# Projection and routing: where the scale and shift of the second normalisation are applied

## What is computed

```python
mod = (silu(c) @ wmod).reshape(8, 6, 1, 512)         # sa, ca, ga, sb, cb, gb per sequence
h = layernorm(x) * (1 + ca) + sa
x = x + ga * attention(h)                            # 16 heads, causal, with output projection
h = layernorm(x) * (1 + cb) + sb                     # the h of this document
shared = relu2(h @ shared_up.T) @ shared_down.T      # 512 -> 1024 -> 512
scores = sigmoid(h @ gate_w.T)                       # 32 experts, 4 chosen per token
routed = sum over the 4 chosen experts of weight * relu2(h @ up[e].T) @ down[e].T
x = x + gb * (routed + shared)
```

## Time and profile before

| | |
|---|---|
| median of 3 runs | 3025.01 us (3016.74 to 3033.07) |
| span of the profiled execution, first to last instruction | 3027.5 us |
| PE busy | 2895.4 us, 96% |
| PEld busy | 2168.3 us, 72% |
| DVE busy | 2179.3 us, 72% |
| POOL busy | 1833.5 us, 61% |
| ACT busy | 1341.6 us, 44% |

### The profile page before, as it was taken

How to read it: one execution, slowest core, us unless ns; L and a number is a source line. 1 busy time by engine, 2 the same in 40 slices (tenths; PEclk the granted TensorE clock), 3 DMA queues, 4 the chain that set the end, 5 groups by cost and what they waited for, 6 DMA issues and landing times.

```text
span 3027.5 us, 49806 instructions
## 1 busy us (share of the span) xinstructions
PE 2895.4 (96%) x16480; PEld 2168.3 (72%) x16480; DVE 2179.3 (72%) x5344; ACT 1341.6 (44%) x2436; POOL 1833.5 (61%) x1077
## 2 busy tenths in 40 slices
PE   8999999999999999999999989999999999989997
PEld 5788888766666666666666677777777787767775
DVE  6555555678787878787877687777777787756664
ACT  2222222156666666666666522233222333226664
POOL 1233222278888888888886256766565666655664
PEclk9999999999999999999999999999999999999998
DMA  7655555756655665566555333332322322238996
GB/s 240 211 187 201 187 180 180 233 114 136 137 124 115 138 138 121 115 139 140 119 117 160 107 97 93 94 112 74 103 79 93 102 85 81 73 107 222 239 245 118
DMA packets 281948, 420.53 MB, mean 139 GB/s; under 512 B 48463, under 2 KB 132687, under 8 KB 281742
## 3 DMA queue, kind: packets, MB, share of 16 engines
q1 hardware_dynamic: 259214, 384.22, 44.9%
q0 software_dynamic: 22528, 33.72, 5.8%
HBM read 263.38 MB, written 153.01 MB: 138 GB/s over the span
## 4 chain that ended last, share of the span: by engine, by line
PE 53%; DVE 14%; POOL 14%; issue 8%; ACT 4%; DMA 4%; another core or an unknown queue 2%; DVEq 1%; POOLq 0%; SPq 0%; ACTq 0%
PE qkv_ps_m L840 12%; PE ffn_ps_m L2191 11%; POOL att_gathered L1105 6%; PE qkv_ps_m L844 6%; POOL att_pt L1098 5%; PE att_ps_o L1330 5%; PE att_ps_p L1386 4%; PE att_ps_s L1304 4%; DMA out<-exp_y,exp_tok_add 2%; PE exp_ps_u L1607 2%; PE exp_ps_y L1623 1%; PE att_ps_s L1361 1%; DVE ffn_att L147 1%; DVE ffn_x L149 1%
## 5 line engine op out<-in xcount | busy, mean ns | idle before, releaser
L247 DVE CUSTOM_DVE_ANT_0 att_ps_s<-att_ps_s,att_causal 128x512 f32<-128x512 f32 (+1 forms) x992 | 469.3, 502 | 175.5 <-PE att_ps_s L1304 171.3
L1166 ACT ACTIVATE att_pt<-att_ps_p 128x512 f32<-128x512 f32 (+1 forms) x1024 | 524.5, 589 | 143.6 <-PE att_ps_p L1389 110.2
L1304 PE MATMUL att_ps_s<-att_ks,att_qs 96*128 96x512 f32 x1488 | 513.4, 373 | 2.2 <-DVE att_lower L253 0.6
L1386 PE MATMUL att_ps_p<-att_qs,att_ks 98*128 98x512 f32 (+3 forms) x1536 | 498.5, 364 | 9.3 <-ACT att_pt L1166 8.0
L1098 POOL TENSOR_TENSOR att_pt<-att_pt 128x1024 f32<-128x1024 f32 (+2 forms) x153 | 331.1, 2164 | 166.6 <-PE att_ps_o L1330 144.8
L1105 POOL TENSOR_TENSOR att_gathered<-att_gathered,att_pt 128x2048 f32<-128x2048 f32 (+1 forms) x92 | 388.1, 4218 | 7.2
L1912 POOL DMA_INDIRECT slot_info<-ffn_info,ffn_slot x256 | 275.9, 1078 | 119.3 <-issue 76.5
L253 DVE TENSOR_REDUCE att_lower<-att_ps_s 128x1 f32<-128x512 f32 x496 | 339.2, 684 | 7.4 <-PE att_ps_s L1304 7.4
L1386 PEld LDWEIGHTS att_ps_p<-att_qs,att_ks 98*128 98x128 f32 x1536 | 272.6, 191 | 82.1 <-issue 34.7
L1304 PEld LDWEIGHTS att_ps_s<-att_ks,att_qs 96*128 96x128 f32 x1488 | 275.7, 191 | 73.3 <-DVE att_rowmax L247 27.7
L577 POOL TENSOR_TENSOR qkv_x<-qkv_x,qkv_mod 128x512 f32<-128x512 f32 x60 | 83.4, 1391 | 371.5 <-DVE qkv_x L671 371.5
(11 more groups left out here) (311 smaller groups left out, 6718.8 us busy)
## 6 DMA issues: line engine op xcount, KB each, us to landing
att_qs<-qk_parts SPq DMA_DIRECT2D x96, 512.0 KB, 6.8
att_ks<-qk_parts SPq DMA_DIRECT2D x96, 512.0 KB, 12.7
qk_parts<-qkv_out_hi SPq DMA_DIRECT2D x128, 256.0 KB, 2.2
qk_parts<-qkv_out_lo SPq DMA_DIRECT2D x128, 256.0 KB, 2.4
qkv_x<-x SPq DMA_DIRECT2D x16, 1024.0 KB, 5.6
v_rows<-qkv_out_v SPq DMA_DIRECT2D x64, 256.0 KB, 2.3
att_vs<-v_rows SPq DMA_DIRECT2D x32, 512.0 KB, 16.1
o_parts<-att_o SPq DMA_DIRECT2D x64, 256.0 KB, 7.9
```

The lines of the kernel that those rows point to most:

```text
L247: dve.tensor_tensor_reduce(part, part, self.causal[:, UNIT - (c1 - c0):UNIT], scale=1.0, scalar=MASKED, op0=ALU.add, op1=ALU.max, accum_ou ...
L1166: act.activation(tile(c)[:, h, col:UNIT], ps_p[(NPROB * prev.g + n) % NP][:, col:UNIT], ACT.Exp, scale=float(HD) ** -0.5).then_inc(exp_don ...
L1304: pe.matmul(bank("s", cur.g, i)[:, 0:c1 - c0], qs[cur.slot][0:STACK, h, t * P:(t + 1) * P], ks[cur.slot][0:STACK, h, c0:c1], start=True, s ...
L1386: last = pe.matmul(part[:, i * (UNIT - col):(i + 1) * (UNIT - col)], ks[prev.slot][:, h + i, kt * P:(kt + 1) * P], qs[prev.slot][:, h + i, ...
```

## The change

TensorE turns rows that are only normalised. ScalarE then scales and shifts the turned tile in its PSUM bank, where a feature is a partition, so `1 + cb` and `sb` are one column each per block of 128 features (four activations a tile, `modulated`), and copies it to `hT_hi` as before. GpSimd multiplies and shifts all four tiles of `h2` behind their turns, for the store to DRAM alone. VectorE's part of that for the last tile goes, and in `norm_first` for all four.

With this the order is changed: GpSimd does `normalise(u + 2)` ahead of `modulate`, and `scatter` in one piece; SyncE stores `h2` of unit u at the start of the body of u, ahead of the wait for the projection and of loading the attention output; the columns `mod_cols` are loaded element by element for every sequence; tiles 0 and 1 are turned behind the second down tile, tile 2 behind the third, and the last one at pair 2 of the last down tile.

```diff
-LINKS = 2 * UT + 1 + STAT_LINKS + ROOT_LINKS + 2
+LINKS = 2 * UT + 1 + STAT_LINKS + ROOT_LINKS
+MOD_FIRST, MOD_EACH = 48, 80
...
             def load_rows():
 
-                for m, j in enumerate((M_GA, M_CB, M_SB)):
-                    sp.dma_start(bridge.mod[:, m, :], mod_dram[0:1, j, :].broadcast_to([P, D])).then_inc(late.mod_in, 16)
+                sp.dma_start(bridge.mod[:, 0, :], mod_dram[0:1, M_GA, :].broadcast_to([P, D])).then_inc(late.mod_in, 16)
+                for m, j in enumerate((M_CB, M_SB)):
+                    sp.dma_start(bridge.mod_cols[:, m, :], mod_dram[0:1, j, :].rearrange("o (k p) -> p (o k)", p=P),
+                                 allow_slow_non_contiguous=True).then_inc(late.mod_in, 16)
...
             def norm_first():
 
                 late.deviation(dve, 0, 0, bridge.mv, bridge.std, bridge.rstd, bridge.tmp)
                 for t in range(UT):
-                    last = dve.tensor_scalar(late.h2[:, t, :], late.x0[:, t, :], bridge.mv[:, t, 0:1], bridge.rstd[:, t:t + 1],
-                                             ALU.subtract, ALU.mult)
...
+                    dve.tensor_scalar(late.h2[:, t, :], late.x0[:, t, :], bridge.mv[:, t, 0:1], bridge.rstd[:, t:t + 1],
+                                      ALU.subtract, ALU.mult).then_inc(late.norm_done, 1)
...
-        TURNS = ((), (0,), (1, 2), ())
-        SCATTERED_AHEAD = TOPK
+        TURNS = ((), (0, 1), (2,), ())
+        LAST_TURN = 2
...
             def store_h2(b, half):
                 u = b * HALVES + half
-                sp.wait_ge(h_done, CREDIT + PT * (u + 1))
-                sp.wait_ge(norm_done, CREDIT + UT * (u + 1))
+                sp.wait_ge(h_done, CREDIT + UT * (u + 1))
...
                 if more:
-                    nb, nhalf = (b, 1) if half == 0 else (b + 1, 0)
...
-                        sp.wait_ge(proj_done, CREDIT + UT * (u + 2))
-                        load_o(b + 1, half)
-                    store_h2(nb, nhalf)
-                    if half == 0 and has_next2:
-                        load_mod(b + 1)
+                    store_h2(b, half)
+                if more and half == 1:
+                    sp.wait_ge(hi_done, CREDIT + UT * (u + 1))
+                    load_mod(b + 1)
+                if b < LAST:
+                    sp.wait_ge(proj_done, CREDIT + UT * (u + 2))
+                    load_o(b + 1, half)
...
             def modulate(b, half):
                 u = b * HALVES + half
-                for t in range(PT):
-                    pool.wait_ge(norm_done, CREDIT + UT * u + t + 1)
+                pool.wait_ge(mod_in, CREDIT + MOD_FIRST + MOD_EACH * (b + 1))
+                pool.sem_inc(mark, 1)
+                for t in range(UT):
+                    pool.wait_ge(tr_done, CREDIT + UT * u + t + 1)
...
             def body(b, half, more):
                 u = b * HALVES + half
-                if u == UNITS - 2:
-                    scatter(u, half, 0, SCATTERED_AHEAD)
+                if b < LAST:
+                    normalise(u + 2)
+                if u >= UNITS - 2:
+                    scatter(u, half)
                 if more:
                     modulate(*((b, 1) if half == 0 else (b + 1, 0)))
-                if half == 0 and not (isinstance(b, int) and b == LAST) or half == 1 and more:
-                    normalise(u + 2)
-                scatter(u, half, SCATTERED_AHEAD if u == UNITS - 2 else 0, UT * TOPK)
+                if u < UNITS - 2:
+                    scatter(u, half)
...
-            def turn(u):
-
+            def turn(u, cols):
+
+                act.wait_ge(mod_in, CREDIT + MOD_FIRST + MOD_EACH * (u // HALVES + 1 if u else 0))
                 for t in range(UT):
                     act.wait_ge(tr_done, CREDIT + UT * u + t + 1)
+                    for k in range(DK):
+                        part = ps_t[t % 2][:, k * P:(k + 1) * P]
+                        last = act.activation(part, part, ACT.Identity, bias=cols[:, 1, k:k + 1], scale=cols[:, 0, k:k + 1])
+                    last.then_inc(modulated, 1)
+                    act.wait_ge(modulated, CREDIT + UT * u + t + 1)
                     act.activation(hT_hi[:, :, t * P:(t + 1) * P], ps_t[t % 2][:, :].rearrange("p (k c) -> p k c", k=DK), ACT.Copy).then_inc(hi_done, 1)
...
                 for t in range(UT):
-                    last = dve.tensor_scalar(h2[:, t, :], xs[:, t, :], mv[:, t, 0:1], rstd[:, t:t + 1],
-                                             ALU.subtract, ALU.mult)
...
-                last.then_inc(dve_own, 1)
-                dve.wait_ge(dve_own, own + 1)
-                dve.tensor_tensor(h2[:, PT, :], h2[:, PT, :], mod[:, 1, :], ALU.mult).then_inc(dve_own, 1)
-                dve.wait_ge(dve_own, own + 2)
-                dve.tensor_tensor(h2[:, PT, :], h2[:, PT, :], mod[:, 2, :], ALU.add).then_inc(norm_done, 1)
+                    dve.tensor_scalar(h2[:, t, :], xs[:, t, :], mv[:, t, 0:1], rstd[:, t:t + 1],
+                                      ALU.subtract, ALU.mult).then_inc(norm_done, 1)
...
             def turn(u, t):
-                if t < PT:
-                    pe.wait_ge(h_done, CREDIT + PT * u + t + 1)
-                else:
-                    pe.wait_ge(norm_done, CREDIT + UT * (u + 1))
+                pe.wait_ge(norm_done, CREDIT + UT * u + t + 1)
                 pe.wait_ge(lo_done, CREDIT + UT * u + t - 1)
...
                     def before_pair(n):
-                        if more and t == PT and 2 * n == UP:
+                        if more and t == PT and n == LAST_TURN:
                             turn(u + 1, PT)
```

More of the change, by code:

```diff
@@ L197, in __init__ @@
         self.q_in, self.v_in, self.m_in = s.sems("q_in", SLOT), s.sems("v_in", SLOT), s.sems("m_in", SLOT)
-        self.pool_own, self.add_done, self.sum_done, self.mark = (s.sem(n) for n in ("pool_own", "add", "sum", "mark"))
+        self.pool_own, self.add_done, self.sum_done = (s.sem(n) for n in ("pool_own", "add", "sum"))
+        self.mark = late.mark
         self.s_done, self.max_done = s.sem("s"), s.sem("max")
@@ L1246, in normalise_first @@
                 dve.wait_ge(late.x_in[0], CREDIT + 16)
-                dve.wait_ge(late.mod_in, CREDIT + 48)
+                dve.wait_ge(late.mod_in, CREDIT + MOD_FIRST)
             def norm_first():
@@ L1811, in body @@
                 if more:
-                    nb, nhalf = (b, 1) if half == 0 else (b + 1, 0)
-                    if half == 0:
-                        has_next2 = not (isinstance(b, int) and b == LAST)
-                    else:
-                        has_next2 = True
-                    if has_next2:
-                        sp.wait_ge(proj_done, CREDIT + UT * (u + 2))
-                        load_o(b + 1, half)
-                    store_h2(nb, nhalf)
-                    if half == 0 and has_next2:
-                        load_mod(b + 1)
+                    store_h2(b, half)
[5 more added lines that the diff above has]
+                    load_o(b + 1, half)
                 if not more:
@@ L1905, in body, with scatter @@
                     pool.iota(relay.iota_i[:, :], pattern=[[1, NK]], base=0, channel_multiplier=0).then_inc(relay.iota_done, 1)
-            def scatter(u, half, first, end):
+            def scatter(u, half):
                 pool.wait_ge(slot_done, CREDIT + u + 1)
                 pool.sem_inc(mark, 1)
-                for j in range(first, end):
+                for j in range(UT * TOPK):
                     pool.indirect_dma_start(
@@ L1975, in body @@
                     root(u + 1)
-                    turn(u + 1)
+                    turn(u + 1, mod_cols)
             steps(act, body)
@@ L2020, in attend @@
                 late.deviation(dve, u, LINKS * u, mv, std, rstd, tmp)
-                own += 2 * UT + 1 + STAT_LINKS + ROOT_LINKS
                 dve.wait_ge(tr_done, CREDIT + UT * u)
```

36 lines of the change are left out of this document (12 added, 24 removed).

## The result

The changed kernel takes 3068.81 us in the median of four runs (3044.78 to 3077.09), the kernel before 3020.88 us in four runs beside it (3015.03 to 3033.07). The ratio is 1.016, its 95% interval 1.013 to 1.0195: 48 us slower, where 29 us faster was forecast. The profiled execution of the changed kernel is its fastest one, 3044.8 us, span 3043.1. The other three took 3061 to 3077 us at a lower mean granted clock (0.977 to 0.980 against 0.982) and have no trace, so what follows explains the fastest run and not the whole 48 us.

The account below looks back on a forecast made before the run. TensorE was taken to bound the kernel, with only its idle and slow time, some 50 us, winnable. Terms 20.5 + 11.4 + 5.5 - 5 - 3 = 29.4 us off the 3025.0 median gave 2996 us, range 2982 to 3018.

Parts of the forecast that it names:

- the 28.5 and 12.6 us: TensorE's waits ahead of turns, for the row GpSimd shifts last and for VectorE's low part, counted as winnable.
- (d): GpSimd modulates four tiles instead of three, behind the split: 3 us lost in all, bounds 0 and 15.
- (e): SyncE's queues, with the earlier store and element-wise column loads: nothing lost, bounds 0 and 3.
- (a): First turns no longer wait for a shifted row, only for VectorE's normalisation: 20.5 us won, 8 left.
- (b): New turn order lets VectorE's low part come in time: 1.2 of 12.6 us left, 11.4 in the sum.
- (f): Clock: slow spells behind TensorE's waits go in three of five units, 5.5 us won, bounds 2 and 8.
- the wait of 3.41 us: Third longest of TensorE's 12 waits for GpSimd's row; forecast to leave 0.6 us after the change.
- ScalarE at its full price: Rival that ScalarE becomes the bound, small operations at 0.78 us: 30 us lost, 3024 us; chance 0.12.
- (c): ScalarE scales and shifts: 0.46 us per small operation, no loop cost, 5 us lost at the start.
- third rival: GpSimd's modulation under VectorE's routing, first 10 us of the up products, delays normalisation: 3053 us; chance 0.12.
- that sign: Sign of a wrong forecast: VectorE's first output-projection sum starting later behind the up products than before.
- The page's rule: Two-port VectorE operations and GpSimd instructions exclude each other; normalisations would wait, (a) leave 18 us, time 3006.

Follow-up runs that it names:

- e5: The kernel before, unchanged, on the first of the experiments' chips, which showed no stalls: 2967.6 us, ratio 1.000.
- e12: Kernel before with four idle VectorE steps ahead of the output projection's sums and without scatters: 3002.4 us, ratio 1.006 to the kernel before.
- e13: Changed kernel with the same four idle VectorE steps ahead of the sums and without scatters: 2994.7 us, ratio 1.003 to the kernel before.
- e16: The kernel before, unchanged, on a later chip that stalls: 3023.6 us, ratio 1.000.
- e17: The changed kernel, unchanged, on the chip of e16: 3034.0 us, ratio 1.0065 to the kernel before.
- first pair: Profiled executions of the kernel before and the changed kernel from the first comparison, whose medians were 3020.88 and 3068.81 us.
- e9: Changed kernel with GpSimd's modulation of the first unit left out: 2970.7 us, ratio 0.999 to the kernel before.
- e6: The changed kernel, unchanged, on the quiet chip of e5: 2983.6 us, ratio 1.005 to the kernel before.
- e8: Changed kernel with scatters ahead of GpSimd's modulation and gate rows loaded apart and earlier: 3044.5 us, ratio 1.025 to the kernel before.
- e2: The kernel before with the scatters left out, on the chip of e5: 2960.4 us, ratio 0.997 to the kernel before.
- e18: The changed kernel with the scatters left out, on the chip of e16: 2970.4 us, ratio 0.983 to the kernel before.

## Why the prediction was wrong

*What bounds the kernel.* TensorE, right, and the waits were counted right. Two steps failed. The first was to take the 28.5 and 12.6 us as the loop's own. They hang on stalls that come before the sum, on some chips; on the quiet chip (e5) the down side loses 2.6 us in all, so next to nothing can be won. The second, which turned the sign in the forecast's own comparison, was to put the up side at nothing, below under (d), (e). A third, smaller one is the 3 us of (d).

*(a), (b), (f).* The mechanism is shown where the sum is late: e12 against e13 18.0 us, e16 against e17 31.1, the first pair 21.3, for a forecast of 20.5 + 11.4 and 5.5 of clock. In the first pair 23.7 of the 23.9 us that are left stand in four units. In two of these the sum began only 1.5 and 1.9 us ahead of the down products and the split then lay on the statistics, in two VectorE waited 2.2 and 3.3 us more for projection tiles between its sums. Taken wrong was the time of a normalisation (median 0.54, not 1.01 us), since in most units VectorE is done before the split begins. The working also has slips too small to matter: the wait of 3.41 us would leave 0.8 and not 0.6, so 8.3 in place of 8 us are left, and ScalarE at its full price gives 3026 and not 3024.

*(c)* was right: 0.43 us for 0.46, no gate product waits in the loop of the first trace (one, 0.4 us, in e17), the start costs 4.5 us for 5.

*(d)* was too small: 3 us for everything, where the first unit alone loses 5.6 net and 8.0 by e9. That is the third rival's mechanism (GpSimd's modulation under VectorE's small steps) in a place I hadn't looked at, the one unit whose routing steps stand between low parts that ScalarE waits for. In the loop the sum comes 1.5 us later behind the up products (27.4 for 25.9 us, e6 and e5), inside the slack, and no run shows what of the change delays it; that sign had been named as one that would make the forecast wrong.

*(d), (e): nothing for the up side.* This is the term that turned the sign: 37.9 us in the first pair, 21.9 in the last, forecast at nothing. I held the scatters' shift of 1 to 4 us to be free (it is 3.6 between e5 and e6: the first from 6.2 to 9.8 us behind the up products' start, the start of the last from 27 to 30) and had not read what ScalarE waits for there.

*The page's rule.* Beside a GpSimd instruction steps of 0.17 us took 1.25 and steps of 0.42 took 1.42, while a sum that reads PSUM keeps its 0.68. The Trainium skill, SBUF — State Buffer, section "Who interferes with whom", says that a VectorE instruction with two SBUF inputs contends with a GpSimd instruction that reads SBUF. It says too that in a two-port mode one of the two blocks for the other's whole instruction. By both the traces agree in the main; a small step with one tensor input waited as well (L300 above, 1.19 us), and no run shows in which mode it ran. The forecast had priced this for the four long normalisations alone and left the many short steps to a rival of chance 0.12; it counts by the number of steps, as e8 shows at full size.

*What stays open.* Which resource the scatters hold, and why only some chips show it. And whether the changed order stalls more by itself, which the 48 us of the first comparison would need. For it: in the first pair ScalarE's idle time ahead of the relu, counted as above, is 160 us against 131. In both pairs 9 and 7 of 14 units lose over 1 us on the up side, against 3 and 3 in the kernel before, and the later scatters reach further into the output projection, which begins at 22.4 us and in which TensorE itself has to wait. Against: in e16 and e17 the same idle time is 141 and 147 us, where the quiet e5 and e6 have 97 and 101, so 44 and 46 us more; with the sum held it is 7 units against 6. And the changed kernel's loss on that chip, 20 us (11 to 29), can't be told from the 15 us (11 to 20) of e6 on the quiet one. So the larger loss of the first comparison, 48 us in four runs, was not seen again. In the kernel before the stalls end up in the down side's 45 us, where the changed order wins part of them back. No run moved the scatters alone on a chip that stalls. No version that computes the whole result was faster than the kernel before by more than its interval.

## What to carry to other kernels

Ask of a wait that you mean to remove what made its producer late, back to the first engine that waits for something the profile can't name: if that is a stall, the gain is there only on a chip that has it. When work moves to GpSimd, count the VectorE instructions that come to lie beside it, not their time; each small one that reads SBUF can cost what is left of a GpSimd instruction, here 1.3 us. Time both kernels on more than one chip before a per cent is believed.

## What the runs showed of the hardware

The same program took 2968 to 3021 us in the median by chip. In the traces of e5 and e16 its third stage, from the first turn to the last unit's down products, takes 934 and 998 us; 60 of these 64 us are on the up and down sides of the 14 units. ScalarE waits up to 10.9 us for a tile whose products are long recorded. Every such wait over 1.3 us (from 1745 to 2655 us) ends behind the unit's first scatter and at most 2.7 us behind the end of its last one, and the five traces without scatters have none. The place in the program matters: from up to down products the ninth and tenth units took 35.6 and 42.0 us in the first trace of the kernel before and 35.6 and 41.6 in e16, and the ninth and twelfth of the changed kernel 40.7 and 42.0, then 40.2 and 42.2 in e17; other units differed. Left out, the scatters give back 8 us on a quiet chip (e2), of which the third stage has only 1 (933 us against 934 in e5), and 64 us on one that stalls (e18 against e17), 55 of them there.
